# A two-layer perceiver with two cross attentions on one core: folds of latent attention computed in the ternary stage, value weights folded into output weights in layer 1's attention, and further reorderings

## What is computed

```python
x = x + L0_xattn(ln(x), ctx)   # A: 16 heads of 16, causal
x = x + L0_attn(ln(x))         # B: gated delta rule, 16 q/k and 32 v heads of 128
x = x + L0_ffn(ln(x))          # C: ternary weights, quantised input, GELU twice
x = x + L1_xattn(ln(x), ctx)   # D
x = x + L1_attn(ln(x))         # E
x = x + L1_ffn(ln(x))          # F: top 2 of 8 LoRA experts
# D, per head h:
q_big = rope((x @ Wq_h.T) @ w_kc_q_h)           # 192
q_r, k_r = q_big @ W_qr_h, rope(ctx) @ W_kr_h   # 64 each
p = softmax(q_r @ k_r.T)
y += ((p @ rope(ctx)) @ w_kc_kv_h.T) @ Wo_h.T
# E, 16 heads in 4 groups g that share keys and values:
v = (x @ W_kv_down) @ W_v_g                     # 64, then 128
y += (softmax(mask(q @ k.T)) @ v) @ W_o_h
```

## Time and profile before

| | us |
|---|---|
| median of 3 runs | 883.21 (881.78 to 892.46) |
| the profiled execution | 887.37 |
| its span | 885.6 |
| stages A, B, C (starts 0, 62.3, 400.9) | 62, 338, 33 |
| stages D, E, F (starts 434.3, 723.2, 810.0) | 289, 86, 76 |

### The profile page before, as it was taken

How to read it: one execution, slowest core, us unless ns; L and a number is a source line. 1 busy time by engine, 2 the same in 40 slices (tenths; PEclk the granted TensorE clock), 3 DMA queues, 4 the chain that set the end, 5 groups by cost and what they waited for, 6 DMA issues and landing times. The chain is left out here.

```text
span 885.6 us, 14636 instructions
## 1 busy us (share of the span) xinstructions
PE 747.6 (84%) x5423; PEld 565.9 (64%) x5424; DVE 510.3 (58%) x1250; ACT 373.2 (42%) x1020; POOL 180.6 (20%) x363
## 2 busy tenths in 40 slices
PE   5856558999999988772479999999999989886998
PEld 3744446887887867560347667666767777664655
DVE  1536665769878873533536665566666425663561
ACT  1504874456456445223225545545555423221220
POOL 1012883156545633000000000000000010000000
PEclk9657868999999999775569999999999999996999
DMA  5003212633133112000393111110201034000000
GB/s 195 1 0 137 109 53 81 226 106 101 28 93 104 22 46 59 24 1 0 113 287 65 22 39 21 26 34 20 40 20 13 7 104 188 1 1 0 1 0 13
DMA packets 44454, 53.21 MB, mean 60 GB/s; under 512 B 29120, under 2 KB 34368, under 8 KB 43136
## 3 DMA queue, kind: packets, MB, share of 16 engines
q1 hardware_dynamic: 43104, 50.16, 18.5%
q0 software_dynamic: 1280, 2.12, 2.3%
HBM read 50.90 MB, written 1.36 MB: 59 GB/s over the span
## 5 line engine op out<-in xcount | busy, mean ns | idle before, releaser
L1606 ACT COPY d_Pt<-bank 128x512 f32<-128x512 f32 x96 | 51.6, 589 | 102.2 <-PE bank L1529 102.2
L1681 DVE TENSOR_REDUCE d_nm<-scores 128x1 f32<-128x1024 f32 x64 | 75.4, 1219 | 20.4 <-PE scores L1522 20.4
L1050 DVE SCALAR_TENSOR_TENSOR b_yc<-b_cpad,b_slab,b_yc 128x256 f32<-128x256 f32 x192 | 79.9, 488 | 0.0
L1618 ACT ACTIVATE d_Pr<-scores,d_negm 128x1024 f32<-128x1024 f32 x64 | 70.7, 1109 | 17.7 <-DVE d_negm L1684 17.7
L1529 PEld LDWEIGHTS bank<-cst,d_Pr 128*128 128x128 f32 x512 | 56.2, 141 | 29.1 <-issue 24.7
L1529 PE MATMUL bank<-cst,d_Pr 128*128 128x128 f32 x512 | 69.2, 278 | 0.4 <-DVE d_Pt L1658 0.4
L1522 PE MATMUL scores<-d_KM,d_Q 64*128 64x512 f32 x256 | 65.4, 630 | 2.0 <-ACT d_Q L1597 2.0
L661 PE MATMUL bank<-xnT,b_slab 128*128 128x256 f32 x256 | 63.9, 401 | 2.1 <-ACT b_cpad L900 2.1
L1542 PE MATMUL bank<-d_Pt,d_KV 128*64 128x128 f32 x1024 | 63.0, 276 | 0.0
L1542 PEld LDWEIGHTS bank<-d_Pt,d_KV 128*64 128x64 f32 x1024 | 55.2, 137 | 7.8 <-issue 5.8
L661 PEld LDWEIGHTS bank<-xnT,b_slab 128*128 128x128 f32 x256 | 51.4, 206 | 10.3 <-issue 2.7
(11 more groups left out here) (327 smaller groups left out, 1551.1 us busy)
## 6 DMA issues: line engine op xcount, KB each, us to landing
b_slab<-in_b_slab SPq DMA_DIRECT2D x16, 520.0 KB, 3.7
b_wz<-in_b_wz SPq DMA_DIRECT2D x16, 256.0 KB, 3.7
b_wo<-in_b_wo SPq DMA_DIRECT2D x16, 256.0 KB, 2.9
d_w<-in_d_w SPq DMA_DIRECT2D x16, 224.0 KB, 2.5
b_DT<-b_cs SPq DMA_DIRECT2D x2, 1536.0 KB, 10.4
f_w<-in_f_w SPq DMA_DIRECT2D x3, 896.0 KB, 10.0
c_w<-in_c_w SPq DMA_DIRECT2D x2, 1024.0 KB, 6.2
d_wo<-in_d_wo SPq DMA_DIRECT2D x1, 2048.0 KB, 8.2
```

What stands on the lines that cost most here:

```text
L1050: last = dve.scalar_tensor_tensor(yc[x][:, ch], src, tap, yc[x][:, ch], ALU.mult, ALU.add)
L1606: act.copy(Pt[g][:].rearrange("p j q -> p (j q)"), TP[g % 2]).then_inc(pt_cp[g % 2], 1)
L1618: act.activation(Pr[b][:, keys], scores[:, 2 * k:2 * k + 2, :].rearrange("p g k -> p (g k)"), ACT.Exp, bias=negm[:, b:b + 1], accum_out=su ...
L1681: last = dve.tensor_reduce(nm2[:, b, k:k + 1], scores[:, 2 * k:2 * k + 2, :].rearrange("p g k -> p (g k)"), AX, ALU.max, negate=True)
```

## The change

1. PE gets filler matmuls (`busy`): 11, 8 and 9 ahead of the layer norm's transposes of stages B, E and F, and 12 ahead of the last `turn_h` of stage B.
2. Stage A: PE follows each unit's transposes with the value matmuls of the unit two before; DVE takes the maxima of the unit four ahead between the copies.
3. Stage B: DVE does `hide` for pairs 2 to 7 and POOL for 0 and 1 alone; ACT does `decays(0)` at the end of turn -2 and all others at the end of turn -1; in every turn ACT turns the previous pair's outputs ahead of `level_y`.
4. Stages C and D: the latents' transposes, the combined key weights of all 16 heads (`keys_tensor`, four groups of 8 matmuls of 64 columns where there were 2 of 128 columns a head) and four of the eight folds (`values_tensor`) move into stage C; three folds stand at the start of D, the last behind `front2` of head 0. ACT does all their copies. The weights come by DMA at the start of C. POOL clears semaphores after its powers.
5. Stage E: values stay at 64 latent numbers (straight from the input), and the value weights of each group are multiplied with its output weights (`fold_values`, `wvo`). The product with the values has 64 rows, two heads side by side in the 128 partitions; the output product has half the matmuls and stands one group later, behind the transposes; DVE's add moves with it.

The core of the diff:

```diff
+        def busy(bank, n):
+
+            for _ in range(n):
+                nc.tensor.matmul(bank[:, 0:P], ones[:], ones[:], start=True, stop=True)
+
+        env["busy"] = busy
+
         def ln_tensor(n):
+            busy(bk[6], {1: 11, 4: 8, 5: 9}.get(n, 0))
...
+            def values(n):
+
+                b, j = n // 4, n % 4
+                pe.wait_ge(tr_cp, n + 1)
+                for m in range(HG):
+                    h = 4 * m + j
...
+            LAG = 2
+            for n in range(4 * B):
+                turn(n)
+                if n >= LAG:
+                    values(n - LAG)
+            for n in range(4 * B - LAG, 4 * B):
+                values(n)
...
+            env["busy"](PJ[0], 12)
...
-                    level_y(i, 0, 0)
-                    level_y(i, 0, 1)
                 for x in range(2):
                     if behind:
                         turn_h(i - 1, x)
                 if solving:
+                    level_y(i, 0, 0)
+                    level_y(i, 0, 1)
+                if solving:
                     level_turn(i, 0, 0)
                     level_turn(i, 0, 1)
-                if i == -1:
-                    decays(2)
-                    decays(3)
...
-                    decays(1)
                 if i == -1:
-                    for k in range(4, PAIRS):
+                    for k in range(1, PAIRS):
...
-                    for k in range(5, PAIRS):
+                    for k in range(2, PAIRS):
...
+            early["latents_tensor"]()
+            for k in range(3):
+                early["keys_tensor"](k, w64)
...
+            early["keys_tensor"](3, w64)
...
+            pe.wait_ge(early["wc_cp"], 4)
             for b in range(B):
+                if b:
+                    pe.wait_ge(tr_cp, 3)
+                for k in (2 * b, 2 * b + 1):
+                    early["values_tensor"](k)
                 turn(b)
+                if b == 0:
+                    pe.wait_ge(early["w_cp"], 2)
                 out(b)
...
+    def load(sp, w64):
+        sp.dma_start(w64[:], a["d_w64"].rearrange("h p n -> p h n")).then_inc(w["w64_in"], 16)
+        for half in range(2):
+            sp.dma_start(wkv[:, :, half, :], a["d_wkv"]).then_inc(w["tail_in"], 16)
+        sp.dma_start(wo[:], a["d_wo"]).then_inc(w["tail_in"], 16)
...
+    def keys_tensor(k, w64):
+
+        nc.tensor.wait_ge(w["w64_in"], 16)
+        if k == 3:
+            nc.tensor.wait_ge(w["wc_cp"], 1)
+        for n in range(8):
+            h, half = 4 * k + n // 2, n % 2
+            last = nc.tensor.matmul(WB[k][0:XQ, n * LAT:(n + 1) * LAT], w64[:, h, half * XQ:(half + 1) * XQ], w64[:, h, X_CQ:],
+                                    start=True, stop=True)
+        last.then_inc(w["wc_mm"], 1)
...
+    def values_tensor(k):
+
+        if k == 0:
+            nc.tensor.wait_ge(w["tail_in"], 48)
+        for hh in range(2):
+            h = 2 * k + hh
+            last = nc.tensor.matmul(FB[k][:, hh * D:(hh + 1) * D], wkv[:, h].rearrange("p t d -> p (t d)"), wo[:, h, :], start=True, stop=True)
+        last.then_inc(w["w_mm"], 1)
...
-                for half in range(2):
-                    last = pe.matmul(FB[0:XQ, TOK + half * P:TOK + (half + 1) * P].rearrange("p (b d) -> p b d", b=B),
-                                     w64[x][:, half * XQ:(half + 1) * XQ],
-                                     w64[x][:, X_CQ:].unsqueeze(1).to_broadcast([X_R, B, LAT]), start=True, stop=True)
+                    last = pe.matmul(FB[:, 0:TOK], w128[x][:, c * X_K:(c + 1) * X_K], xnT[:, c, :], start=(c == 0), stop=(c == DC - 1))
...
-            def fold(k):
-
-                if k == 0:
-                    pe.wait_ge(tail_in, 48)
-                pe.wait_ge(q_done, k + 2)
-                for hh in range(2):
-                    h = 2 * k + hh
-                    last = pe.matmul(FB[:, hh * D:(hh + 1) * D], wkv[:, h].rearrange("p t d -> p (t d)"), wo[:, h, :], start=True, stop=True)
-                last.then_inc(w_mm, 1)
...
+            def fold_values(n):
+                if n >= 2:
+                    pe.wait_ge(x_acc, n - 1)
+                for k in range(NP):
+                    for hh in range(2):
+                        last = pe.matmul(Y[hh * LAT:(hh + 1) * LAT, k * D:(k + 1) * D], wv[:, n, :], wo[:, n * E_REP + 2 * k + hh, :],
+                                         start=True, stop=True)
+                last.then_inc(vo_mm, 1)
+
+            def output(n):
+                pe.wait_ge(pv_cp, B * (n + 1))
+                pe.wait_ge(vo_cp, min(n + 2, E_KV))
+                if n:
+                    pe.wait_ge(x_acc, n)
+                for b in range(B):
+                    for k in range(NP):
+                        last = pe.matmul(Y[:, b * D:(b + 1) * D], oT[b][:, k, :], wvo[:, n, k, :], start=(k == 0), stop=(k == NP - 1))
+                last.then_inc(y_mm, 1)
...
+                if n:
+                    output(n - 1)
                 for b in range(B):
                     pe.wait_ge(tr_cp, B * n + b + 1)
-                    pe.matmul(SC[b], v[:, b, n * E_V:(n + 1) * E_V], PT[b][:].rearrange("p j q -> p (j q)"),
-                              start=True, stop=True).then_inc(pv_mm, 1)
-
-                pe.wait_ge(pv_cp, B * (n + 1))
-                if n:
-                    pe.wait_ge(x_acc, n)
-                for b in range(B):
-                    for j in range(E_REP):
-                        last = pe.matmul(Y[:, b * D:(b + 1) * D], oT[b][:, j, :], wo[:, n * E_REP + j, :],
-                                         start=(j == 0), stop=(j == E_REP - 1))
-                last.then_inc(y_mm, 1)
+                    for hh in range(2):
+                        last = pe.matmul(SC[b][SIDE[hh], 0:NP * P].rearrange("p (k q) -> p k q", k=NP), v[:, b, :], PT[b][:, hh::2, :],
+                                         start=True, stop=True)
+                    last.then_inc(pv_mm, 1)
+            output(E_KV - 1)
```

231 lines of the change are left out of this document (137 added, 94 removed).

## The result

The changed kernel takes 842.4 us (median of 4 runs, 841.2 to 851.0) against 885.6 for the kernel before in the same comparison: a ratio of 0.9505, 95% interval 0.9463 to 0.9548. The forecast was 828 with a range of 813 to 850, so the time lies in the range, 14 us above the number named. The profiled execution took 841.2 us, its span is 839.4, against 887.4 and 885.6.

The account below looks back on a forecast made before the run. PE, busy 84% of the span, was taken as the bound, through its instruction list and its clock. Terms summed to -56 us: 887.4 to 831 for the profiled execution, so a median of 828, range 813 to 850.

Parts of the forecast that it names:

- Stage A: Value matmuls interleaved with groups of four transposes, ending near 50 instead of 55.1: -5 us, at most -14, at worst -4.
- Start of B: Fillers lift the clock for the 16 convolution matmuls, -3.5 us; mask adds and decays shared out anew, -1.5.
- Steady pairs of B: ACT turns b_hT first, so PE's 1.06 us wait goes in each of 7 pairs: -7.4 us, at least -4.
- End of B: 12 fillers in a wait for DVE make the last 16 output matmuls warm: -3.3 us, 0 if cold.
- Stage C: Key matmuls moved in ahead of the main matmuls, +2 us (-1.2 to +4.7), and value folds, +0.5: +2.5 together.
- Rival 4: Stage C: key weights landing after 409.8 delay PE us for us; chance 0.02 over 2% slower, 0.02 gain only lost.
- Start of D: Latents' transposes and copies gone, first query tile earlier, -6.8 us; first score period shorter, -2.9.
- D's loop: A fold (1.07, 8 heads) and second weight product (0.61, 14 heads) gone, -17.1 us; late reciprocal transfer, +0.5.
- Rival 2: D's loop is not PE's: the reciprocal's transfer or DVE bounds the half, giving back 9 us, 837; chance 0.10.
- Stage E: Halved output product moved and folds added, groups 13.2 apart instead of 16.14: -9 us (-5 to -11).
- Start of F: 9 fillers bring 16 matmuls from 6.24 us cold to 3.4 warm: -2.6 us (+1 to -4).
- the rule that I weighed for B's start: DVE's 3.8 us of added mask adds would block POOL's solver, making the sharing term about +2 instead of -1.5.

Follow-up runs that it names:

- c_w64_early: The changed kernel with the 1 MB of key weights loaded at the end of stage B instead of in stage C: 833.0 us.
- e_output_behind_pv: The changed kernel with each stage E group's output product put back behind the same group's product with the values, folded weights kept: 844.9 us.

## Why the prediction was right, and where it was not

The sign, the size of D's part and the range were right. By the steps of the prediction:

- *Stage A*, -5 forecast, -8.9 measured, and -6.8 to -9.5 over all the traces. The mechanism is the one described: each group of four transposes is followed by 8 value instructions. I worked it out at the low clock only. In the trace the first three groups of 8 took 0.96 to 1.14 us and the last 1.7 to 1.8, since PE had the upper level again for part of 30 to 36 us; that is the bound of -14 reached in part. No run tested it alone.
- *Start of B*, -3.5 for the clock and -1.5 for the sharing. The sum is nearly right (the first output product of B came 4.1 earlier), and that is luck, since both reasons are wrong. The clock term assumed that fillers ahead of the transposes last up to the products behind them. They don't: the gaps of 1.72 and 0.77 us between were enough for it to fall. For the sharing I had said that the solver's chain and not ACT's copies ends the stretch; with the gathered decays it is ACT's copy, with a wait of 3.16, and the 3.4 us that the sharing gains ahead of it are lost there. Of the 4.1 us, 1.5 come from ScalarE's new order, and 2.6 from rows that were at the low level in the kernel before and not here.
- *Steady pairs of B*, -7.4 forecast for seven turns. Measured: -1.5 ahead of the first output product, -1.5 in the first distance, 0 in the second, -0.12 in each of the third and fourth, and -1.4 and -0.9 in the last two; the fifth is +2.0, by the clock, and the sum -3.5. The step that failed is that a wait of 1.06 is worth 1.06 in every turn: it is worth 1.5 where nothing else is near, and 0.12 in the steady pairs. I found the wait for b_hT, and looked for what would be late next at one place only, the predicated copies, where DVE and PE had 0.6 and 0.7 of slack. The chain that counts goes from DVE's list through its convolution and ACT's silu to the transposes of b_qkv. In the kernel before the silu ends 0.25 us ahead of these transposes, and where PE waits for it, they start 0.14 behind its end: 0.11 of slack. The bound for a loop rests on the shortest slack of all that PE waits for in it, not on the one that I had looked at.
- *End of B*, -3.3 forecast. From the last output product's start to the stage's end 4.5 for 6.8, -2.4, of which the fillers are 1.7 by the run without them. In five of the twelve traces with these fillers the products stayed at the low level, and the end took 6.1 for 6.8.
- *Stage C*, +2.5 forecast, +5.6 measured. The power came earlier, as said. The weights landed 8.4 us after the issue and not 6.2. The row that I took is the median of two loads of the same size, issued one behind the other, that took 5.0 and 7.4. They go into 128 partitions; this one goes into 64, and others follow it. No run separates the two, so why it took 8.4 (8.3 to 9.2 over the traces, and 9.2 with the longest C, 39.9) stays open. And the cold end of my range was the true one: behind its wait PE did the keys at the low level. I had the weights land "behind the transposes", but did not say what PE does in between: it stood there for 6.46 us. Rival 4's mechanism was real, and its deadline of 409.8 was too late: the weights landed 8.7 us into the stage, ahead of that deadline (9.2), but the 48 key instructions behind them take 7.9 more, and the input's transposes came 7.4 us after the input.
- *Start of D*, -6.8 and -2.9 forecast, -9.0 and -2.0 measured: near the warm end, since the folds keep PE busy there.
- *D's loop*, -17.1 + 0.5 forecast, 207.2 for 221.9 over 14 heads, -14.7, measured. The fold and the second weight product were on the path with their full 1.07 and 0.61: the shortest periods, 14.63, are just that much below 16.30. The price of the late reciprocal was 2.4 instead of 0.5: the transfer, 3.4 to 4.0 before, took 3.4 to 4.7 here, so in some heads it ends after DVE wants it and in most it does not. Rival 2 was true in those heads. In the trace of c_w64_early they are ten of the 14, and the sum is 210.
- *Stage E*, -9 forecast, -6.2 measured. The period was forecast as 13.2 and is 13.42. The three groups gave -8.0; the start cost +1.4 (2.1 forecast). The tail is the term that failed: +0.4 for -2.2. Its value product and half of its output product are cheaper, but another output product, that of the group before, now stands in it, at the low clock (3.62 us), and I had not counted it; in e_output_behind_pv, where it does not, the tail is 1.5 shorter. In six other traces the first group took 13.4 instead of 15.0 and E 78.6 to 79.2, which would be -7.6 to -8.2.
- *Start of F*, -2.6 forecast and measured; but the products took 5.4, not 3.4, and the rest came from the shorter transposes and the router's product (1.03 for 1.85). When the products were brought to the upper level, DVE's mask took all but 0.5 of it, and in two of three traces the clock fell behind that wait. That the whole term came out at -2.6 is luck.

On the rule that I weighed for B's start: six mask adds on DVE took 7.39 us, and beside them four of POOL's solver operations took 1.14 to 1.16 us each where their neighbours of the same size take 0.27 to 0.31, as three did before the change:
```profile
107.40 0.28 POOL L645 TENSOR_TENSOR b_S<-b_S,b_tmp 64x50 f32<-64x50 f32 x1
107.75 1.14 POOL L643 TENSOR_TENSOR b_tmp<-b_G,b_S 64x54 f32<-64x54 f32 x1
...
115.15 0.27 POOL L643 TENSOR_TENSOR b_tmp<-b_G,b_S 64x56 f32<-64x56 f32 x1
```
That agrees with what the Trainium skill, "SBUF — State Buffer", "Who interferes with whom", says of two SBUF inputs against a GpSimd read. It is not seen in the time: PE waited 3.16 us for ACT's b_cpad there and not for the solved blocks.
